# A three-layer graph network on one core: the order of the units in the third layer

## The chip, the cores and the metric

The kernel runs on one core of one Trainium2 chip. The metric is the device time in microseconds (us) of one execution. An execution is told by five engines that run side by side, each through its own list of instructions in order, and that wait for one another at semaphores: PE (TensorE, matmuls), DVE (VectorE), ACT (ScalarE), POOL (GpSimd, which here also issues the indirect DMAs) and SP (SyncE, which issues the plain DMAs).

## The reference

A graph of 20,000 nodes with 512 features each and 5,000 edges, sorted by their destination. Three layers of the same form, then the input is added back and normalized:

```python
h, residual = x, 0.0
for Wl, bl, Wr, g, b in params:          # three layers, weights 512 x 512
    msg = h[src]
    s = segment_sum(msg, dst)
    agg = s / maximum(cnt, 1.0)
    h = residual + agg @ Wl.T + bl + h @ Wr.T
    h = layer_norm(h, g, b)
    h = where(h >= 0, h, a_prelu * h)
    residual = h
out = layernorm(x + h)
```

## The kernel before, in words

The rows of a layer lie in 157 tiles of 128 rows (NT). Edge slots fill the first 40 tiles (ET): at most 127 edges each, so only these 40 tiles need the sum over messages. Tiles are worked through in pairs, called units: 20 **edge units** and 59 **plain units** (the last of them has one tile), 79 units a layer (UL), 237 in all. The list ORDER gives the sequence of a layer's units, the same in all three layers: 20 plain units (LEAD), then nineteen times an edge unit with two plain units behind it, then the last edge unit and the plain unit of one tile. In this text a unit's **position** is its place in its layer, 0 to 78, and "the row of position p" is the time on PE from the first transpose of that unit to the first transpose of the next.

Every engine walks over a counter T, the number of a unit, and does its part for units near T. The lists are written out by hand, so the order on an engine is fixed:

- PE (`tensor_program`): `turn` transposes the unit ahead (T+1) into ps_t (L373, 8 transposes for two tiles). Then `sum_messages` for tile 0 of the unit ahead if it is an edge unit (L385), `product_self` of tile 0 of unit T (L393, 12 matmuls), `sum_messages` for tile 1, `product_self` of tile 1, and for an edge unit `product_mean` for both tiles (L393, 12 matmuls each on sT). A plain unit is 8 transposes and 24 matmuls, an edge unit has 16 summing matmuls and 24 matmuls more.
- ACT (`scalar_program`): `square` of the second tile of T-1 (L499), `variance` (L509), `take_high` of T+1 (L490, from ps_t), in the third layer `out_norm` of T-4 (L552), `fill` of the bias into ps_z for T+1 (L519), in the third layer `out_square` of T-3 (L545), then `take_sum_high` of an edge unit (L528) and `square` of the first tile of T.
- POOL (`gpsimd_program`): `root` (L650, a power, and in the third layer L654 for the output), in the third layer `put_out` of T-5, two indirect DMAs that write the output (L662), then `gather_x`, `gather_messages` of T+3 if that is an edge unit (two indirect DMAs of 128 rows, L639).
- DVE (`vector_program`): `prelu` and in the third layer `out_sum` of T-3 (L784, L826), `take_sum_low` (L818), `carry` and `take_low` of T+1 (L745), `out_mean` (L833), `normal` and `add_shift` of T-1 (L757, L778), and `compare` for an edge unit at T+3 (L793, L795).
- SP (`sync_program`): `load_h` of T+3 (L283), `load_residual` in the third layer (L311), `load_rowtab` of T+5 (L293), `store_h` of T-3 (L300).

What ties them: `turn` of a unit waits until DVE has taken the low part of the one before it out of ps_t (`low`), `product_self` waits for `fill`, `fill` and `out_norm` stand behind one another on ACT, and `out_norm` waits for the L654 of POOL in the same step:

```python
act.wait_ge(o_move, u.pos + 1)      # out_norm, ACT
pool.wait_ge(o_done, u.o_ahead + j + 1)   # put_out, POOL
pe.wait_ge(m_in[j], 16 * (u.eno + 1))     # sum_messages, PE
```

The messages of layers two and three are gathered from the h that the layer before has stored in DRAM; `gather_messages` of the first edge unit of a layer waits until all of it is stored.

Of the kernel before, what the change touches and what calls it, by code (L numbers as in the profile page):

```python
# [15 lines left out]
L = 3  # L16
# [12 lines left out]
def build_program(nc, x, wT, bl, g, b, a_prelu, ident_in, const_in, edge_cols_in, edge_last_in, edge_rows_in,  # L29
# [5 lines left out]
    NT = -(-(N + ET) // P)  # L35
# [3 lines left out]
    edge_units = [(t, t + 1) for t in range(0, ET, 2)]  # L39
    plain_units = [tuple(range(t, min(t + 2, NT))) for t in range(ET, NT, 2)]  # L40
    UL = len(edge_units) + len(plain_units)
    UNITS = L * UL


    LEAD = len(plain_units) - 2 * len(edge_units) + 1
    assert LEAD >= 20
    ORDER = plain_units[:LEAD]
    for i, tiles in enumerate(edge_units):
        ORDER += [tiles, *plain_units[LEAD + 2 * i:min(LEAD + 2 * i + 2, len(plain_units) - 1)]]
    ORDER += plain_units[-1:]  # L50
    assert len(ORDER) == UL
    AHEAD = [sum(len(t) for t in ORDER[:i]) for i in range(UL)]
    EDGE_AT = [l * UL + ORDER.index(tiles) for l in range(L) for tiles in edge_units]

    class Unit:

        def __init__(self, no):
            self.no = no
            self.exists = 0 <= no < UNITS
            if not self.exists:  # L60
                return
            self.l, self.pos = divmod(no, UL)
            self.tiles = ORDER[self.pos]
            self.n = len(self.tiles)
            self.edge = self.tiles[0] < ET
            self.ahead = NT * self.l + AHEAD[self.pos]
            self.upto = self.ahead + self.n
            self.r2, self.r3 = no % 2, no % 3

            self.eno = len(edge_units) * self.l + self.tiles[0] // 2  # L70
            self.ring, self.lap = self.pos % OB, self.pos // OB
            self.o_ahead, self.o_upto = self.ahead - NT * (L - 1), self.upto - NT * (L - 1)

    def uses(ring, n, below):

        return len(range(ring, below, n))
# [7 lines left out]
    with ExitStack() as ctx:  # L84
# [3 lines left out]
        def sem(name):  # L88
            return ctx.enter_context(nc.semaphore(name))


        OB = 6
# [80 lines left out]
        edge_no, first, run = room[1][:, 0:P], room[1][:, P:2 * P], room[1][:, 2 * P:3 * P]  # L173
# [29 lines left out]
        BATCHES = -(-ET // BATCH)  # L203
        KNOWN_SLOT = [EDGE_AT[BATCH // 2 * b] - 4 for b in range(BATCHES)]

        EARLY, HALF = 18, 11
        NODE_SLOT = [2 + t if t < EARLY else EDGE_AT[(t - EARLY) // 2] + 1 + t % 2 for t in range(ET)]
        PLACES = EDGE_AT[1:HALF] + [T + i for T in EDGE_AT[HALF:len(edge_units)] for i in range(3)] + [UL, UL + 1, UL + 2]
        PUT_SLOT = PLACES[:ET]
# [3 lines left out]
        SRC_AHEAD = 6  # L213
        assert all(NODE_SLOT[t] < KNOWN_SLOT[t // BATCH] < PUT_SLOT[t] for t in range(ET)) and TABLE_SLOT + 3 < LEAD - 1 and PUT_SLOT[0] > TABLE_SLOT + 4
        assert len(PUT_SLOT) == ET and PUT_SLOT[-1] + 2 < EDGE_AT[len(edge_units)] - SRC_AHEAD

# [32 lines left out]
        o_put = [[sem(f"o_put{i}_{j}") for j in range(2)] for i in range(OB)]  # L249
# [3 lines left out]
        def rows(dram, u):  # L253
            return dram[P * u.tiles[0]:P * (u.tiles[0] + u.n), :].rearrange("(j p) d -> p j d", p=P)


        def sync_program(sp):
# [17 lines left out]
            def load_h(u):  # L275
                if u.l == 0:
                    return
                source = u.no - UL
                sp.wait_ge(turned, u.no - 2)
                sp.wait_ge(h_stored[source % 3], 16 * (source // 3 + 1))  # L280
                if u.no - 3 < UL:
                    sp.wait_ge(xp_stored[u.r3], 16 * uses(u.r3, 3, UL))
                sp.dma_start(hin[u.r3][:, 0:u.n, :], rows(h_dram[u.l - 1], u)).then_inc(h_in[u.r3], 16)  # L283
# [47 lines left out]
            for T in range(-5, UNITS + 3):  # L331
                for stage_, ahead in ((store_x, 2), (load_h, 3), (load_residual, -1), (load_rowtab, 5), (store_h, -3)):
                    u = Unit(T + ahead)
                    if u.exists:
                        stage_(u)
                for w, at in W_SLOT.items():
                    if T == at - 4:
                        load_weight(w)
                if T == TABLE_SLOT + 2:
                    sp.wait_ge(table_done, 3)  # L340
                    sp.dma_start(slot_dram[0:P * P, :].rearrange("(t p) c -> t (p c)", p=P),
                                 table_int[:, 0, :]).then_inc(slot_stored, 16)
                    sp.dma_start(slot_dram[P * P:NT * P, :].rearrange("(t p) c -> t (p c)", p=P),
                                 table_int[0:NT - P, 1, :]).then_inc(slot_stored, 16)
# [123 lines left out]
        def scalar_program(act):  # L468
# [52 lines left out]
            def take_sum_high(u, j):  # L521
# [3 lines left out]
                if u.eno > 0:  # L525
                    before = Unit(EDGE_AT[u.eno - 1])
                    act.wait_ge(z_ready, before.ahead + j + 1)
# [71 lines left out]
        def gpsimd_program(pool):  # L599
# [68 lines left out]
            for T in range(-3, UNITS + 6):  # L668
# [5 lines left out]
                for stage_, ahead in ((gather_x, 3), (gather_messages, 3), (find_source, SRC_AHEAD)):  # L674
                    u = Unit(T + ahead)
# [18 lines left out]
                        add_diagonal(w)  # L694
            for ring in range(OB):
                for j in range(2):
                    pool.wait_ge(o_put[ring][j], 16 * len([p for p in range(ring, UL, OB) if len(ORDER[p]) > j]))  # L697


        def vector_program(dve):  # L700
# [256 lines left out]
        with nc.Block() as block:  # L957
            block.sync(sync_program)
            block.tensor(tensor_program)
            block.scalar(scalar_program)  # L960
            block.gpsimd(gpsimd_program)
            block.vector(vector_program)
# [57 lines left out]
```

## Time and profile before

| | us |
|---|---|
| median of 3 runs | 2044.36 (2043.84 to 2045.36) |
| profiled execution, its own time | 2046.63 |
| profiled execution, span from first to last instruction | 2044.8 |
| PE busy | 1978.4 (97%) |
| DVE busy | 1601.2 (78%) |
| ACT busy | 1212.6 (59%) |
| POOL busy | 929.1 (45%) |

The span begins with set-up of tables and ends with the drain of the last units. The first transpose of the third layer stands at 1352.3 us. The busy time of PE is an upper figure, since matmuls overlap and their ends are modelled; the number to read is the time from a unit's first transpose to the next one's. In a timeline row the bracket at the end gives how long the engine stood idle before it and who released it.

### The profile page before, as it was taken

The page shows a single profiled execution, that of the slowest core. Times are in us where ns is not written, and L with a number is a line of the kernel's source. Part 1 is how long each engine was busy: PE and PEld are TensorE (multiplying, and loading weights), DVE is VectorE, ACT ScalarE, POOL GpSimd, SP SyncE. Part 2 cuts the span into 40 slices and gives each one's busy share as a digit, 9 for nine tenths or more (in the row PEclk, how much of TensorE's full clock was granted, in tenths as well). Part 3 has the DMA queues.
Part 4 walks back from the last instruction along what each step waited for, and adds up shares of the span by engine and source line. Part 5 has one row for each costly group of instructions (what it writes and reads, how often), then busy time and mean ns, then how long its engine had stood idle before and what let it go on. Part 6 is the DMA issues. An engine that isn't in the chain of part 4 may idle for free. (4 is left out here: it accounts for less than half of the span.)

```text
span 2044.8 us, 30402 instructions
## 1 busy us (share of the span) xinstructions
PE 1978.4 (97%) x10149; PEld 1653.5 (81%) x10149; DVE 1601.2 (78%) x2619; ACT 1212.6 (59%) x2643; POOL 929.1 (45%) x885
## 2 busy tenths in 40 slices
PE   6899999999999999999999999999999999999993
PEld 4778888888888888888888888887788888888882
DVE  7668787777777777777777777779998888888884
ACT  3775545555444455544444444458877777777774
POOL 2566655555665321233333333214555545555554
PEclk8999999999999999999999999999999999999997
DMA  5567676666666565444444444455666655566652
GB/s 185 179 214 270 206 228 227 209 224 211 206 207 200 170 170 171 165 155 155 155 145 147 152 155 155 135 176 197 228 223 211 214 208 206 211 216 213 210 186 90
DMA packets 181073, 387.66 MB, mean 190 GB/s; under 512 B 20117, under 2 KB 20562, under 8 KB 180918
## 3 DMA queue, kind: packets, MB, share of 16 engines
q1 hardware_dynamic: 142358, 272.06, 39.4%
q0 software_dynamic: 38560, 113.67, 17.3%
q8 instruction: 81, 1.33, 0.3%
q14 instruction: 74, 0.61, 0.1%
HBM read 221.07 MB, written 164.79 MB: 189 GB/s over the span
## 5 line engine op out<-in xcount | busy, mean ns | idle before, releaser
L393 PE MATMUL ps_z<-w_hi,hT_hi 128*128 128x512 f32 x1884 | 764.5, 406 | 5.2 <-ACT ps_z L519 5.0
L393 PE MATMUL ps_z<-w_hi,hT_lo 128*128 128x512 f32 x1884 | 739.8, 393 | 0.0
L393 PE MATMUL ps_z<-w_lo,hT_hi 128*128 128x512 f32 x1884 | 739.1, 392 | 0.0
L650 POOL TENSOR_TENSOR rstd<-veps,minus_half 128x2 f32<-128x2 f32 (+1 forms) x240 | 239.9, 1000 | 890.1 <-ACT veps L509 890.0
L745 DVE TENSOR_TENSOR hT_lo<-ps_t,hT_hi 128x1024 fp32r<-128x1024 f32 (+1 forms) x237 | 287.9, 1215 | 341.3 <-ACT hT_hi L490 338.7
L519 ACT COPY ps_z<-bias_rows 128x512 f32<-128x512 f32 x471 | 276.8, 588 | 370.1 <-DVE y L757 359.6
L499 ACT ACTIVATE junk<-ps_z 128x512 f32<-128x512 f32 x471 | 277.9, 591 | 318.8 <-PE ps_z L393 318.6
L393 PEld LDWEIGHTS ps_z<-w_hi,hT_lo 128*128 128x128 f32 x1884 | 354.1, 188 | 78.9
L393 PEld LDWEIGHTS ps_z<-w_hi,hT_hi 128*128 128x128 f32 x1884 | 355.4, 189 | 74.5 <-issue 8.1
L393 PEld LDWEIGHTS ps_z<-w_lo,hT_hi 128*128 128x128 f32 x1884 | 355.6, 189 | 66.8
L757 DVE SCALAR_TENSOR_TENSOR y<-ps_z,rstd,gain 128x512 f32<-128x512 f32 x471 | 330.1, 742 | 4.5 <-POOL rstd L650 4.5
L784 DVE SCALAR_TENSOR_TENSOR hout<-y,slope 128x1024 f32<-128x1024 f32 (+1 forms) x237 | 301.4, 1272 | 0.0
L778 DVE TENSOR_TENSOR y<-y,shift 128x1024 f32<-128x1024 f32 (+1 forms) x237 | 290.4, 1225 | 8.1
L373 PEld LDWEIGHTS ps_t<-ident,hin 128*128 128x128 f32 x1884 | 220.5, 141 | 38.6 <-issue 8.9
L373 PE MATMUL ps_t<-ident,hin 128*128 128x128 f32 x1884 | 246.6, 274 | 4.7 <-DVE hT_lo L745 4.7
L490 ACT CAST hT_hi<-ps_t 128x1024 fp32r<-128x1024 f32 (+1 forms) x237 | 234.6, 990 | 19.4 <-PE ps_t L373 19.2
L662 POOL DMA_INDIRECT out<-o_sb,node_put x157 | 165.3, 1053 | 68.2 <-issue 53.3
L616 POOL DMA_INDIRECT hin<-in_x,node_get x157 | 157.1, 1001 | 69.8 <-issue 36.2
L393 PE MATMUL ps_z<-w_hi,sT_lo 128*128 128x512 f32 x480 | 188.2, 392 | 0.0
L393 PE MATMUL ps_z<-w_lo,sT_hi 128*128 128x512 f32 x480 | 187.9, 391 | 0.0
L393 PE MATMUL ps_z<-w_hi,sT_hi 128*128 128x512 f32 x480 | 187.9, 391 | 0.0
L810 DVE SCALAR_TENSOR_TENSOR sumT<-over,sumT,ps_s 128x128 f32<-128x128 f32 x468 | 130.9, 342 | 37.9 <-PE ps_s L385 37.8
(131 smaller groups left out, 1898.7 us busy)
## 6 DMA issues: line engine op xcount, KB each, us to landing
h_scratch<-hout SPq DMA_DIRECT2D x156, 512.0 KB, 3.4
hin<-h_scratch SPq DMA_DIRECT2D x156, 512.0 KB, 4.0
x_by_slot<-hin SPq DMA_DIRECT2D x78, 512.0 KB, 3.2
o_sb<-x_by_slot SPq DMA_DIRECT2D x78, 512.0 KB, 4.5
rowtab<-edge_row_table SPq DMA_DIRECT2D x60, 256.0 KB, 3.5
stage<-in_WrT SPq DMA_DIRECT2D x3, 1024.0 KB, 8.5
stage<-in_WlT SPq DMA_DIRECT2D x3, 1024.0 KB, 7.0
hin<-in_x,node_get POOLq DMA_INDIRECT x157, 3.6
```

The source lines that it names most:

```text
L373: mm = pe.transpose(ps_t[:, j, k * P:(k + 1) * P], hin[u.r3][:, j, k * P:(k + 1) * P], ident[:])
L393: mm = pe.matmul(acc, a[:, k, :], ww[:, k, :], start=False, skip_group_check=True, stop=stop and k == KC - 1 and a is a_lo)
L490: nc.scalar.copy(hT_hi[u.r2][:, 0:u.n].rearrange("p j k n -> p (j k n)"), ps_t[:, 0:u.n, :].rearrange("p j d -> p (j d)")).then_inc(high, 1)
L499: nc.scalar.activation(junk[j][:], ps_z[u.r2][:, j, :], ACT.Square, accum_out=ssq[u.r2][:, j:j + 1]).then_inc(squared, 1)
L519: nc.scalar.copy(ps_z[u.r2][:, j, :], bias_rows[:, u.l, :]).then_inc(filled, 1)
L616: pool.indirect_dma_start(hin[u.r3][:, j, :], None, x, bass.IndirectOffsetOnAxis(node_get[:, t:t + 1], 0)).then_inc(x_in[u.r3][j], 16)
L650: nc.gpsimd.tensor_tensor(rstd[(T - 1) % 2][:, at], veps[(T - 1) % 2][:, at], minus_half[:, at], ALU.pow).then_inc(rstd_done, 1)
L662: pool.indirect_dma_start(out, bass.IndirectOffsetOnAxis(node_put[:, t:t + 1], 0), o_sb[u.ring][:, j, :], None, bounds_check=N - 1, oob_is ...
L745: nc.vector.tensor_tensor(hT_lo[u.r2][:, 0:u.n].rearrange("p j k n -> p (j k n)"), ps_t[:, 0:u.n, :].rearrange("p j d -> p (j d)"), hT_hi[ ...
L757: nc.vector.scalar_tensor_tensor(y[u.r2][:, j, :], ps_z[u.r2][:, j, :], rstd[u.r2][:, j:j + 1], gain[:, u.l, :], ALU.mult, ALU.mult).then_ ...
L778: nc.vector.tensor_tensor(y[u.r2][:, 0:u.n, :], y[u.r2][:, 0:u.n, :], moved, ALU.add).then_inc(shifted, 1)
L784: nc.vector.scalar_tensor_tensor(hout[u.r3][:, 0:u.n, :], y[u.r2][:, 0:u.n, :], slope[:, 0:1], y[u.r2][:, 0:u.n, :], ALU.mult, ALU.max).th ...
```

## The change

Layers one and two keep their order. The third layer gets its own: 8 plain units, then each edge unit with two or three plain units behind it in turn (E P P, E P P P, ten times), then the plain unit of one tile. The positions of edge units go from 20, 23, 26 ... 77 to 8, 11, 15, 18 ... 74. Since the same tile now stands at other positions in layers two and three, `load_h` looks up at which unit number the layer before made it (MADE_AT), and AHEAD becomes a list for each layer.

```diff
+    def order(lead):
+        left, among = len(plain_units) - lead - 1, len(edge_units)
+        first = [lead + max(min(2 * i, left), left * i // among) for i in range(among + 1)]
+        units = plain_units[:lead]
+        for i, tiles in enumerate(edge_units):
+            units += [tiles, *plain_units[first[i]:first[i + 1]]]
+        return units + plain_units[-1:]
+
     LEAD = len(plain_units) - 2 * len(edge_units) + 1
     assert LEAD >= 20
-    ORDER = plain_units[:LEAD]
...
+    ORDERS = [order(LEAD)] * (L - 1) + [order(8)]
+    AHEAD = [[sum(len(t) for t in units[:i]) for i in range(UL)] for units in ORDERS]
+    MADE_AT = [{tiles[0]: l * UL + pos for pos, tiles in enumerate(units)} for l, units in enumerate(ORDERS)]
+    EDGE_AT = [MADE_AT[l][tiles[0]] for l in range(L) for tiles in edge_units]
...
-            self.tiles = ORDER[self.pos]
+            self.tiles = ORDERS[self.l][self.pos]
...
-            self.ahead = NT * self.l + AHEAD[self.pos]
+            self.ahead = NT * self.l + AHEAD[self.l][self.pos]
...
-                source = u.no - UL
+                source = MADE_AT[u.l - 1][u.tiles[0]]
```

Three places on the engines show what moves. First POOL at the start of the third layer; L650/L655 is the root, L654/L659 the move for the output, L662/L667 puts a unit out (the number after o_sb is the position modulo 6), L639/L644 gathers the messages of an edge unit, one DMA a tile. Before, the first gather of the layer stands behind the thirteenth put, that of position 12:

```order
L650 TENSOR_TENSOR rstd1<-veps1,minus_half 128x4
L654 TENSOR_TENSOR omove1<-oneg1,rstd1 128x2
L662 DMA out<-o_sb0,node_put 20000x512 x2
L639 DMA msg0<-h2_scratch,src_slot 128x512
L639 DMA msg1<-h2_scratch,src_slot 128x512
```

With the change it stands behind the first put, that of position 0:

```order
L655 TENSOR_TENSOR rstd0<-veps0,minus_half 128x4
L659 TENSOR_TENSOR omove1<-oneg1,rstd0 128x2
L667 DMA out<-o_sb0,node_put 20000x512 x2
L644 DMA msg0<-h2_scratch,src_slot 128x512
L644 DMA msg1<-h2_scratch,src_slot 128x512
L655 TENSOR_TENSOR rstd1<-veps1,minus_half 128x4
```

The gather of the first edge unit has moved up by twelve units. Second, POOL further on, from the second gather of the third layer to the third. Before, three groups of root, move and put stand between any two gathers:

```order
L639 DMA msg1<-h2_scratch,src_slot 128x512
L650 TENSOR_TENSOR rstd1<-veps1,minus_half 128x4
L654 TENSOR_TENSOR omove2<-oneg2,rstd1 128x2
L662 DMA out<-o_sb1,node_put 20000x512 x2
...
L662 DMA out<-o_sb2,node_put 20000x512 x2
...
L662 DMA out<-o_sb3,node_put 20000x512 x2
L639 DMA msg0<-h2_scratch,src_slot 128x512
```

With the change there are four at this place, and three at the next:

```order
L644 DMA msg1<-h2_scratch,src_slot 128x512
L655 TENSOR_TENSOR rstd0<-veps0,minus_half 128x4
L659 TENSOR_TENSOR omove5<-oneg5,rstd0 128x2
L667 DMA out<-o_sb4,node_put 20000x512 x2
...
L667 DMA out<-o_sb5,node_put 20000x512 x2
...
L667 DMA out<-o_sb0,node_put 20000x512 x2
...
L667 DMA out<-o_sb1,node_put 20000x512 x2
L644 DMA msg0<-h2_scratch,src_slot 128x512
```

The gather belongs to the unit three places on, so where three plain units follow an edge unit it stands behind the step of the first plain one, and where two follow, behind the step of the edge unit. Third, ACT at the end of PE's work, the step of the last unit but one. Before, that unit's neighbour is an edge unit, whose message sums are cast (L528) between the squares:

```order
L528 CAST sT_hi<-sumT 128x512
L499 ACTIVATE junk,ssq<-ps_z 128x512
L528 CAST sT_hi<-sumT 128x512
L499 ACTIVATE junk,ssq<-ps_z 128x512
L509 ACTIVATE veps<-ssq,eps 128x4
L490 CAST hT_hi<-ps_t 128x512
```

With the change the last four units are plain ones:

```order
L550 ACTIVATE stage,ssq<-o_sb,oneg 128x512 x2
L524 COPY ps_z<-bias_rows 128x512
L504 ACTIVATE junk,ssq<-ps_z 128x512 x2
L514 ACTIVATE veps<-ssq,eps 128x4
L495 CAST hT_hi<-ps_t 128x512
```

The casts of the message sums have gone from the end of ACT's list; its number of instructions is the same.

## Rows read from the trace of the kernel before

**Rows 1.** The page, busy time, share of the span and instructions of PE.
```profile
PE 1978.4 (97%) x10149; PEld 1653.5 (81%) x10149; DVE 1601.2 (78%) x2619; ACT 1212.6 (59%) x2643; POOL 929.1 (45%) x885
```

**Rows 2.** Busy time by stretch: us; PE, PEld, DVE, ACT, POOL; PEclk, DMA, GB/s.
```profile
763.70:827.10 63.40, 63.40 (x321) 53.35 (x320) 49.55 (x52) 36.95 (x80) 12.19 (x16) 1.00 0.52 179
1407.40:1478.60 71.20, 66.76 (x322) 52.87 (x321) 64.85 (x101) 63.02 (x141) 37.49 (x41) 1.00 0.68 225
1486.20:1498.20 12.00, 9.91 (x48) 8.56 (x49) 10.55 (x18) 10.53 (x23) 6.43 (x8) 0.86 0.78 298
1516.40:1524.50 8.10, 8.10 (x49) 7.11 (x48) 7.96 (x18) 6.98 (x16) 3.59 (x4) 1.00 0.65 225
1524.50:1536.30 11.80, 11.80 (x57) 9.84 (x56) 11.40 (x22) 7.91 (x18) 7.12 (x6) 1.00 0.58 182
1536.30:1542.66 6.36, 6.36 (x33) 5.34 (x32) 4.17 (x6) 5.58 (x12) 3.27 (x4) 1.00 0.77 258
1542.70:1963.10 420.40, 420.40 (x2177) 356.82 (x2176) 376.58 (x705) 327.74 (x705) 221.91 (x224) 1.00 0.61 210
```

**Rows 3.** PE's timeline, first transposes of positions 7, 20 and 21: start us, us.
```profile
1394.44 1.03 PE L373 MATMUL ps_t<-ident,hin 128*128 128x128 f32 x8
...
1486.16 1.07 PE L373 MATMUL ps_t<-ident,hin 128*128 128x128 f32 x8 [0.25 <-DVE hT_lo L745]
1489.32 2.05 PE L385 MATMUL ps_s<-same,msg 128*128 128x128 f32 x8 [2.09 <-issue]
...
1491.59 0.63 PE L393 MATMUL ps_z<-w_lo,hT_hi 128*128 128x512 f32 x1
...
1498.24 1.03 PE L373 MATMUL ps_t<-ident,hin 128*128 128x128 f32 x8
```

**Rows 4.** Waits from 1401 to 1500 us: us in total, times, longest us.
```profile
ACT o_sb L552 <- POOL omove L654: 11.7, 13, 2.7
...
PE ps_z L393 <- ACT ps_z L519: 5.0, 11, 0.7
```

**Rows 5.** ACT's timeline, start us, us, in for positions 7, 16 and 17.
```profile
1397.75 1.00 ACT L490 CAST hT_hi<-ps_t 128x1024 fp32r<-128x1024 f32 x1
...
1462.00 1.00 ACT L490 CAST hT_hi<-ps_t 128x1024 fp32r<-128x1024 f32 x1
...
1469.23 1.00 ACT L490 CAST hT_hi<-ps_t 128x1024 fp32r<-128x1024 f32 x1
```

**Rows 6.** POOL's timeline, first put's end and the first gather of layer three.
```profile
1394.27 0.98 POOL L662 DMA_INDIRECT out<-o_sb,node_put  x1 [0.30 <-issue]
...
1482.24 1.98 POOL L639 DMA_INDIRECT msg<-h_scratch,src_slot  x1 [0.30 <-issue]
...
1485.73 1.07 POOL L650 TENSOR_TENSOR rstd<-veps,minus_half 128x4 f32<-128x4 f32 x1
```

**Rows 7.** Line L639, landing of its DMAs: the first two of layer three.
```profile
DMA to landing us min/median/max: 6.8/6.9/7.0
```

**Rows 8.** Line L639, landing of its DMAs: the other 38 of layer three.
```profile
DMA to landing us min/median/max: 3.4/4.2/5.6
```

**Rows 9.** POOL's timeline, second plain unit of one block.
```profile
1540.87 0.98 POOL L662 DMA_INDIRECT out<-o_sb,node_put  x1 [0.30 <-issue]
1544.57 1.39 POOL L650 TENSOR_TENSOR rstd<-veps,minus_half 128x4 f32<-128x4 f32 x1 [2.72 <-ACT veps L509]
```

**Rows 10.** ACT's timeline at the same place.
```profile
1537.43 0.99 ACT L490 CAST hT_hi<-ps_t 128x1024 fp32r<-128x1024 f32 x1
...
1544.39 0.99 ACT L490 CAST hT_hi<-ps_t 128x1024 fp32r<-128x1024 f32 x1
```

**Rows 11.** ACT's timeline at the end, its last wait for PE.
```profile
2009.10 0.60 ACT L499 ACTIVATE junk<-ps_z 128x512 f32<-128x512 f32 x1 [2.03 <-PE ps_z L393]
...
2009.82 0.30 ACT L509 ACTIVATE veps<-ssq,eps 128x4 f32<-128x4 f32 x1
```

**Rows 12.** PE's timeline, its last matmul.
```profile
2011.40 0.39 PE L393 MATMUL ps_z<-w_hi,hT_lo 128*128 128x512 f32 x1
```

More of the change, by code:

```diff
@@ L42, in build_program @@
     UNITS = L * UL
+    def order(lead):
[5 more added lines that the diff above has]
+        return units + plain_units[-1:]
     LEAD = len(plain_units) - 2 * len(edge_units) + 1
     assert LEAD >= 20
-    ORDER = plain_units[:LEAD]
[L48 to L53, printed above, removed]
+    ORDERS = [order(LEAD)] * (L - 1) + [order(8)]
+    AHEAD = [[sum(len(t) for t in units[:i]) for i in range(UL)] for units in ORDERS]
+    MADE_AT = [{tiles[0]: l * UL + pos for pos, tiles in enumerate(units)} for l, units in enumerate(ORDERS)]
+    EDGE_AT = [MADE_AT[l][tiles[0]] for l in range(L) for tiles in edge_units]
     class Unit:
@@ L696, in gpsimd_program @@
                 for j in range(2):
-                    pool.wait_ge(o_put[ring][j], 16 * len([p for p in range(ring, UL, OB) if len(ORDER[p]) > j]))
+                    pool.wait_ge(o_put[ring][j], 16 * len([p for p in range(ring, UL, OB) if len(ORDERS[L - 1][p]) > j]))
         def vector_program(dve):
```

## The prediction

> **What bounds the kernel now.** I read the page first: PE is busy for 1978.4 of 2044.8 us [rows 1], so the most that any order can give is the time in which PE waits or runs slowly. Next I read the table of busy time by stretch, cut at first transposes. Ten plain units of the second layer take 63.4 us with PE busy throughout, 6.34 us each; ten plain units of the third layer, positions 9 to 18, take 71.2 us, 7.12 us each, with PE busy for 66.8 of them; one block of an edge unit and two plain ones in the third layer takes 8.1 + 11.8 + 6.4 = 26.3 us, and the next sixteen blocks take 420.4, again 26.3 each, all with PE busy throughout [rows 2]. So the third layer is bound by PE once edge units are mixed in, and by something else in its run of plain units.
>
> What that is: in the run ACT is busy for 63.0 us of ten units and DVE for 64.9, 6.30 and 6.49 a unit, both near PE's 6.34. The engines wait besides: ACT's `out_norm` (L552) waited for POOL (L654) 13 times, 11.7 us in all, 0.9 a unit, and PE waited for ACT's `fill` (L519) 11 times, 5.0 us in all [rows 4]. ACT's work and its wait make 7.2 a unit, and its timeline shows that step: from one `take_high` to the next it is 7.23 us [rows 5]. That is the bound: ACT in order, with a wait for POOL inside. In a block with an edge unit ACT is busy for 7.0 + 7.9 + 5.6 = 20.5 us of 26.3 and DVE for 8.0 + 11.4 + 4.2 = 23.5 [rows 2], so even with 0.9 of waiting in each of three steps ACT has 3 us to spare, which is what a later plain unit can use.
>
> **What is removed.** The first transpose of position 7 starts at 1394.44, that of position 20, the first edge unit, at 1486.16 [rows 3]: 91.7 us for 13 plain units, which at 6.34 would be 82.4. Excess: **9.3 us**. The row of position 20 lasts from 1486.16 to 1498.24, 12.1 us, where an edge row later takes 8.1 [rows 2, 3]. Excess: **4.0 us**, and it has two halves: 2.09 us of waiting ahead of the summing matmuls (L385), and slow matmuls right behind it, 0.63 instead of 0.39 us [rows 3]; the granted clock of the stretch is 0.86 of full [rows 2], part of it at 1.2 instead of 2.4 GHz. The wait is for the messages: POOL issued the gather at 1482.24, the DMAs landed 6.8 to 7.0 us after issue, which is 1489.2, and PE started at 1489.32 [rows 3, 6, 7]. Together 13.3 us. Positions 0 to 6 keep their order, and show no excess worth counting. All other rows of the layer already run at PE's rate.
>
> **What is added or moved.** No instruction is added; PE's, ACT's, DVE's, POOL's and SP's work is the same in number. Four places can cost.
>
> *The first edge unit, now at position 8.* The lag of ACT behind PE has grown to 1397.75 - 1394.44 = 3.3 us at position 7 [rows 3, 5], and PE is not yet held by it. POOL's first put ends at 1394.27 + 0.98 = 1395.25; the gather comes 0.3 later, at 1395.55 [rows 6]. With 7.0 us of landing the messages are there at 1402.6. PE asks for them after the transposes of position 8, at 1394.44 + 6.34 + 0.9 = 1401.7. That is a wait of **0.9 us** in place of 2.1; with the later gathers' 4.2 us of landing [rows 8] it would be none. The gathers keep POOL for 3.5 us (1482.24 to 1485.73, [rows 6]), so the next root is about 1.4 late and ACT with it; PE then stands in a row of 8.1 and one of 11.8 us, which take up most of that. I add 0.3. Sum **+1.2**; bounds 0 and all of the old price of this place, 4.0 with its slow matmuls and 1.2 of delay in the row ahead, 5.2. I take a value near the lower end, because the first gather's own row gives 0.9 and because behind a wait of half the length I expect no slow matmuls.
>
> Here a page of the Trainium skill bears on the sum. "DMA: Bandwidth & Descriptors", section "Anatomy of one DMA", gives a GpSimd DMA about 2.0 us plus its bytes over 436 GB/s, 2.6 us for these 256 KB as an estimate; by it the messages would be there early and this place would cost 0.3 instead of 1.2. The trace does not agree: the median here is 4.2 and the first two took 6.8 and 7.0 [rows 7, 8], so I keep the rows.
>
> *The ten blocks with three plain units.* The third plain unit brings a step of 7.1 to 7.2 us against a row of 6.34, so it adds 0.8 of lag. In the block shown, `take_high` stands 1537.43 - 1536.30 = 1.1 us behind the first transpose of the second plain unit and 1544.39 - 1542.66 = 1.7 behind that of the next unit [rows 2, 10]. In these blocks the gather also moves to the step of the first plain unit: POOL ends its put at 1541.85 [rows 9], the gather's 0.3 and 3.5 us end at 1545.65, and the root which started at 1544.57 [rows 9] starts 1.1 late. The lag at the third plain unit becomes 1.7 + 1.1 = 2.8, under the 3.3 that did not hold PE, and the edge row of 8.1 and the row of 11.8 behind it take it away. The messages: issued at 1542.15, with 4.2 us of landing there at 1546.4, with 7.0 at 1549.2; PE asks at 1542.66 + 6.34 + 0.9 = 1549.9. So **0**; bounds 0 and 0.5 a block (the mean of PE's waits for `fill`, 5.0 / 11, [rows 4]), 5 in all. I take the lower end, for the margins of 0.5 and of 0.7 us or more. What hides both is that margin of one row of PE.
>
> *Loads, row tables and h.* SP's loads of h look up the same or an earlier position of layer two for plain tiles, and one 3 to 12 later for edge tiles, which is stored by then too: an edge unit of position 8 was made at position 20 of 79. The row table of the first edge unit is asked for five units ahead as before. DVE's comparing for it falls into the run, 1 us where DVE idles 0.6 a unit (7.12 less 6.49, [rows 2]); counted in the 0.3 above. Cost 0.
>
> *The end.* Before, the last unit but one is an edge unit. ACT waits for its product (2.03 us, [rows 11]) and starts `variance` (L509) at 2009.82; PE's last matmul ends at 2011.79 [rows 11, 12], 2.0 later, and 33.0 us remain from there to the end. Now the last rows are three plain ones behind one of 11.8. ACT's lag there is 1.1, 1.7 and, at the last unit, 2.5; its step of 7.1, less 0.6 for the one-tile unit, puts that `variance` 2.3 + 6.5 = 8.8 us behind the last first transpose, while PE needs 0.5 + 5.4 + 2.7 = 8.6. So `variance` starts 0.2 after PE's end instead of 2.0 before it, and the drain is longer by **+2.1**. Bounds 0 (the drain hangs on POOL alone) and 4 (one more us in each of two steps).
>
> **Sum.** -13.3 + 1.2 + 0 + 0 + 2.1 = **-10.0 us**. Against the profiled execution: span 2044.8 to 2034.8, its own time 2046.6 to 2036.6. The median of the runs lies 2.3 under that execution's own time, so the forecast is 2044.4 - 10.0 = **2034.4 us**.
>
> **Rivals.** A measurement of this kernel can tell about 0.2%, 4.1 us, from no change.
>
> (a) *All is gained*: the messages land in 4.2 us and the drain is no longer, -13.3: 2031.1. For it: 38 of 40 gathers landed within 5.6 us. Against it: the first pair is the one moved, and the step of 7.1 at the end.
>
> (b) *POOL's late root is passed on.* If each of the ten longer blocks passes its 1.1 us and the third unit's 0.8 to PE, and nothing takes them up, the price is 19 us: 2053. Halfway (only what exceeds the margin of 0.5) it is 10 x 1.4 = 14: 2048, within 0.2%. Against it: DVE and ACT idle for 2 us and more in every block. With a few tenths a block it gives 2037 to 2040.
>
> (c) *The slower one: the messages come late in the longer blocks.* The gather there has 7.7 us from issue to PE's asking, 12 in the shorter ones. If the landing took 9.8 us, PE would wait 2.1 and run slowly behind each wait, 4.0 a block as at position 20: 40 less 10, 2074. It is slower from 1.0 us a block, a landing over 8.7. Against it: 5.6 is the longest of 38 and 7.0 of all [rows 7, 8]. For the slow matmuls behind each wait speaks the rule in "TensorE: Matmul & The Clock Gate" of the Trainium skill, section "HAM oscillation": repeated waits for a DMA send PE back to its slower clock each time. The row of 0.63 us agrees for the one wait here.
>
> (d) *The run is slow wherever it stands*: the time that ACT and POOL need for 59 plain units is only moved. Then nothing is won: 2044. Against it: the sixteen blocks with PE never idle.
>
> **How the numbers follow.** Forecast, 2032.5 to 2037: 0.55. (a): 0.15. (b) in tenths, 2037 to 2040.2: 0.14; (b) in full or (d), within 0.2%: 0.09. (b) at its worst or (c), slower by over 0.2%: 0.04; a gain beyond (a), 0.03. So faster 0.87, same 0.09, slower 0.04. The range takes in (a), and on the other side the bounds of the first edge unit (4 more) and part of the end: 2030.9 to 2039.5.
>
> **What would show it.** Positions 8 to 18 of the third layer in rows of 6.34, 8.1 and 11.8 us, with the one wait ahead of L385 under 1.5 us and no matmuls of 0.63 behind it; blocks of 26.3 and 32.6 us; PE's last matmul 12 us earlier; a drain of 35 us. The forecast is wrong if PE waits for `fill` or for messages in the longer blocks, or if the drain is 33 us or over 37.

## The result, and the profile after

The changed kernel takes 2036.35 us in the median of 6 runs (2035.68 to 2037.35) against 2044.7 of the kernel before (2043.84 to 2046.96); the ratio is 0.9956, 95% interval 0.9946 to 0.9967. That is 8.35 us less where 10.0 was forecast, inside the range. The profiled executions differ by more: the span falls from 2044.8 to 2033.9, by 10.9 us.

Of the page of the changed kernel, the line that answers to [rows 1]:

```profile
PE 1973.3 (97%) x10149; PEld 1651.9 (81%) x10149; DVE 1600.5 (79%) x2619; ACT 1212.3 (60%) x2643; POOL 929.4 (46%) x885
```

The busy table of the changed kernel, columns as in [rows 2]: the first edge unit's row (position 8), the row behind it, one block of an edge unit and three plain ones, and everything from the first transpose of position 11 to that of position 74:

```profile
1400.64:1409.17 8.53, 8.42 (x50) 7.21 (x50) 7.92 (x13) 7.96 (x17) 4.86 (x5) 1.00 0.75 272
1409.17:1420.97 11.80, 11.80 (x57) 9.84 (x56) 11.63 (x23) 10.36 (x24) 6.42 (x7) 1.00 0.63 216
...
1427.30:1460.00 32.70, 32.70 (x170) 27.67 (x169) 29.00 (x54) 25.76 (x57) 16.64 (x18) 1.00 0.57 198
...
1427.30:1957.50 530.20, 530.20 (x2738) 449.43 (x2737) 482.33 (x883) 425.85 (x922) 284.71 (x289) 1.00 0.64 215
```

PE is never idle from position 11 to position 74, and the granted clock is full throughout. The block of four units (positions 11 to 14) takes 32.7 us, which is 26.3 and one row of 6.35. The first edge unit's row is 8.53 us long where 8.14 is PE's own. I added up, for each row from the first transpose of position 1 to that of position 78, what it takes above PE's own time (6.35; 1.79 more for an edge unit's summing; 5.44 more behind an edge unit). The sum is 13.5 us in the kernel before and 0.8 after: **12.7 us gone**. The drain, from the end of PE's last matmul to the end of the span, grew from 33.1 to 34.4 us: **1.4 us given back**. The two make 11.3. The third layer also began 0.2 us earlier, and the row of position 78, which the sum leaves out, is 0.5 us longer than PE's own, most of it a wait for `fill`; that makes the 10.9 of the spans. The wait:

```profile
1996.48 0.47 PE L398 MATMUL ps_z<-w_hi,hT_hi 128*128 128x512 f32 x1 [0.28 <-ACT ps_z L524]
```

The messages at position 8, on PE and on POOL of the changed kernel:

```profile
1400.64 1.05 PE L378 MATMUL ps_t<-ident,hin 128*128 128x128 f32 x8
1401.52 1.06 PE L390 MATMUL ps_s<-same,msg 128*128 128x128 f32 x8
```

```profile
1395.42 1.00 POOL L644 DMA_INDIRECT msg<-h_scratch,src_slot  x1 [0.30 <-issue]
1396.73 1.91 POOL L644 DMA_INDIRECT msg<-h_scratch,src_slot  x1 [0.30 <-issue]
1398.65 1.58 POOL L655 TENSOR_TENSOR rstd<-veps,minus_half 128x4 f32<-128x4 f32 x1
```

PE sums the messages at once: the wait of 2.09 us of [rows 3] is gone, not halved. The gather begins at 1395.42, where the prediction put it (1395.55), and PE asks 6.1 us later. The first of the two gathers landed 3.5 us after its issue, the second 8.1; PE asks for the second one 4.0 us after the first. What is left of 0.4 us stands behind ACT, whose `out_norm` waited for the root that the gather had held up:

```profile
1400.55 1.52 ACT L557 ACTIVATE o_sb<-o_sb,omove,rstd 128x512 f32<-128x512 f32 x2 [1.93 <-POOL omove L659]
```

In the longer blocks POOL's step is the forecast one. The gather and the root behind it in the first of these blocks (positions 11 to 14; the messages are those of position 15), and ACT's wait for the root:

```profile
1453.18 1.02 POOL L644 DMA_INDIRECT msg<-h_scratch,src_slot  x1 [0.30 <-issue]
1454.50 1.91 POOL L644 DMA_INDIRECT msg<-h_scratch,src_slot  x1 [0.30 <-issue]
1456.43 1.58 POOL L655 TENSOR_TENSOR rstd<-veps,minus_half 128x4 f32<-128x4 f32 x1
```

```profile
1458.32 1.52 ACT L557 ACTIVATE o_sb<-o_sb,omove,rstd 128x512 f32<-128x512 f32 x2 [1.93 <-POOL omove L659]
```

ACT waits 1.93 us in place of 0.88, 1.05 more (1.1 forecast), and PE does not notice. The time from the gather's issue to PE's first summing matmul is 7.8 us in the longer blocks (7.6 in the first) and 10.5 behind the shorter ones (9.3 behind the first); in the kernel before it was 11.8 nearly everywhere. Landing, of the 38 gathers behind the first pair, took 4.2 us in the median, 8.6 at most:

```profile
DMA to landing us min/median/max: 3.4/4.2/8.6
```

In the kernel before the longest behind the first pair was 5.6 us [rows 8]. The long ones now belong to the second gather of a pair: in the first three of the longer blocks the first gather landed in 3.4 to 3.6 us and the second in 8.3 to 8.6. PE asks for the second 4 us later than for the first, so neither made it wait.

At the end, ACT's `variance` and PE's last matmul, to be read beside [rows 11, 12]:

```profile
1998.97 0.30 ACT L514 ACTIVATE veps<-ssq,eps 128x4 f32<-128x4 f32 x1
```

```profile
1999.06 0.39 PE L398 MATMUL ps_z<-w_hi,hT_lo 128*128 128x512 f32 x1
```

`variance` starts 0.5 us before PE's end; before it was 2.0 before it. That is 1.5 us, and the drain is 1.4 longer.

### The profile page after: what moved, and what is told of

It reads as the page before. It is cut to its first block and busy times, and to the rows that moved or that the text cites. A ratio compares the mean times of both kernels' runs of the same rounds, so it can differ in the third digit from the quotient of the medians.

```text
span 2033.9 us, 30402 instructions
## 1 busy us (share of the span) xinstructions
PE 1973.3 (97%) x10149; PEld 1651.9 (81%) x10149; DVE 1600.5 (79%) x2619; ACT 1212.3 (60%) x2643; POOL 929.4 (46%) x885
## 5 line engine op out<-in xcount | busy, mean ns | idle before, releaser
L655 POOL TENSOR_TENSOR rstd<-veps,minus_half 128x2 f32<-128x2 f32 (+1 forms) x240 | 240.4, 1002 | 881.2 <-ACT veps L514 881.0
L667 POOL DMA_INDIRECT out<-o_sb,node_put x157 | 167.3, 1066 | 66.5 <-issue 49.8
L557 ACT ACTIVATE o_sb<-o_sb,omove,rstd 128x512 f32<-128x512 f32 x157 | 119.6, 809 | 74.6 <-POOL omove L659 74.6
```

What stands on the lines that cost most here:

```text
L655: nc.gpsimd.tensor_tensor(rstd[(T - 1) % 2][:, at], veps[(T - 1) % 2][:, at], minus_half[:, at], ALU.pow).then_inc(rstd_done, 1)
L667: pool.indirect_dma_start(out, bass.IndirectOffsetOnAxis(node_put[:, t:t + 1], 0), o_sb[u.ring][:, j, :], None, bounds_check=N - 1, oob_is ...
```

## The experiments

There were twelve runs, two of them of the unchanged kernels for comparison, and one a repeat. Theory A is the prediction's: ACT's step of 7.1 us, in order and with the wait for POOL inside, holds PE in a run of plain units, and the first edge unit pays 4 us when it comes at the end of such a run. Theory B puts all of the gain on the first edge unit.

**The run's length: 14 plain units first.**

```diff
-    ORDERS = [order(LEAD)] * (L - 1) + [order(8)]
+    ORDERS = [order(LEAD)] * (L - 1) + [order(14)]
```

> The changed kernel with 14 plain units ahead of the first edge unit of the third layer in place of 8. Theory A (the run: from position 8 on each plain unit ahead of the first edge unit costs PE some 0.7 us, because ACT's step of 7.1 us exceeds PE's row of 6.34, and the first edge unit costs up to 4 us more when it comes at the end of such a run): rows of 7.0 to 7.3 us at positions 9 to 13, 4.4 us of excess there, and 1 to 4 us at the first edge unit; 5 to 8 us over the changed kernel's 2036.4, so 2041.5 to 2044.5. Theory B (the gain is only the first edge unit's wait and slow matmuls, which come after a long run and grow with it): about 2036 to 2038.5, rows of the run near 6.4.

Measured: 2043.71 us (ratio to the kernel before 0.9987, 0.9977 to 0.9997). The stretch of positions 9 to 13, then the first edge unit's row, with PE's wait in it:

```profile
1407.95:1444.04 36.09, 33.47 (x162) 26.43 (x161) 33.50 (x54) 30.90 (x70) 20.58 (x21) 1.00 0.67 225
1444.04:1454.75 10.71, 8.42 (x49) 7.18 (x49) 9.23 (x14) 9.19 (x20) 6.38 (x8) 1.00 0.75 275
```

Five rows take 36.1 us, 7.2 each, as forecast by A (7.0 to 7.3); the summed excess is 7.5 us, 4.6 of it at positions 8 to 13 and 2.6 at the first edge unit. B, which expects rows near 6.4, falls: 6.8 us of excess come back with six plain units, of 12.7. The time, 7.4 us above the changed kernel's 2036.35 in another job, agrees.

**5 plain units first.** The same edit with 5.

> The changed kernel with 5 plain units first in place of 8. Theory A: positions 0 to 7 have no excess in either order, so there is nothing to gain but the 0.4 us of position 8; the first gather now stands where POOL must wait for the last stores of layer two, which can hold the roots by 1 to 4 us. Within 2 us of the changed kernel, PE's rows from position 5 on at its rate with at most 2 us of excess at positions 3 to 6.

Measured: 2036.10 us (0.9959, 0.9944 to 0.9974), beside 2036.19 of the changed kernel in the same job. The excess is 0.4 us, all at position 1. The 0.4 of position 8 is gone, the first gather did not hold PE visibly (1360 to 1400 us has PE busy for 40.0), and there was nothing else to win. That agrees with the prediction's reading that positions 0 to 7 cost nothing worth counting.

**The first edge unit alone.** In the kernel before, the first gather of the third layer is issued three units earlier.

```diff
-                for stage_, ahead in ((gather_x, 3), (gather_messages, 3), (find_source, SRC_AHEAD)):
+                for stage_, ahead in ((gather_x, 3), (gather_messages, 3), (gather_messages, 6), (find_source, SRC_AHEAD)):
                     u = Unit(T + ahead)
                     if u.exists:
+                        first = u.l == L - 1 and u.tiles[0] == 0
+                        if stage_ is gather_messages and first != (ahead == 6):
+                            continue
                         stage_(u)
```

> The kernel before, with one edit: the gather of the first edge unit of the third layer is issued six units ahead in place of three. Theory A: the wait of 2.1 us at the first edge unit and the slow matmuls behind it (1.9 us) go, but the run of 9.3 us stays, and the gather's 3.5 us on POOL now delay one root inside the run, 1 to 2 us; 2 to 4 us under the kernel before, 2040.5 to 2042.5. Theory B: 8 us under the kernel before, near 2036.5.

Measured: 2043.46 us (0.9983, 0.9974 to 0.9993), against 2046.64 in that job. Positions 9 to 18, and the row of position 20:

```profile
1408.31:1479.41 71.10, 66.77 (x322) 52.89 (x321) 64.71 (x101) 63.05 (x141) 41.57 (x43) 1.00 0.72 233
1486.97:1495.15 8.18, 8.18 (x48) 7.16 (x49) 8.04 (x13) 7.28 (x17) 4.37 (x5) 1.00 0.70 247
```

That is 3.2 us less, where A had 2 to 4; the time itself lies above the 2040.5 to 2042.5 expected, since the kernel before stood at 2046.64 in this job and not at 2044.7. The first edge unit's excess is gone whole, 4.0 us, clock and all, and the run's is untouched: ten rows take 71.1 us, in [rows 2] 71.2. The summed excess is 9.5. So the two terms of the prediction, 9.3 and 4.0, have these sizes, and the second can be taken away without the first. The delay of a root that I had expected inside the run did not show; the two gathers took POOL 1.0 us each here.

**ACT's wait filled.** In the kernel before, `square` of the first tile stands right behind `take_high` in positions 5 to 18, and no longer at the end of the step.

```diff
+                early = u.exists and u.l == L - 1 and 5 <= u.pos < LEAD - 1
+                if early:
+                    square(u, 0)
                 old = Unit(T - 4)
                 if old.exists:
                     out_norm(old, 0)
...
-                if u.exists:
+                if u.exists and not early:
                     square(u, 0)
```

> The kernel before, with one edit: for positions 5 to 18 of the third layer ACT squares the first tile of its unit right behind take_high, ahead of out_norm, where it waits for POOL 0.5 to 0.9 us now, in place of at the end of its step. The work is the same. Theory A (ACT in order with the wait for POOL inside sets 7.1 us): the step falls to DVE's 6.5 us, rows of the run of 6.5 in place of 7.1, 5 to 7 us under the kernel before, 2037.5 to 2040. Rival (DVE, busy for 6.49 us a unit, with its own waits sets the row): the row stays within 0.2 us of 7.1, and the time within 1.5 us of 2044.7.

Measured: 2037.49 us (0.9952, 0.9935 to 0.9969). Positions 12 to 18, seven rows:

```profile
1426.99:1473.13 46.14, 45.87 (x225) 37.45 (x224) 44.82 (x71) 44.50 (x99) 24.21 (x29) 1.00 0.74 245
```

ACT's timeline in one of these steps:

```profile
1463.69 1.00 ACT L490 CAST hT_hi<-ps_t 128x1024 fp32r<-128x1024 f32 x1
1464.59 0.60 ACT L499 ACTIVATE junk<-ps_z 128x512 f32<-128x512 f32 x1
...
1465.42 1.52 ACT L552 ACTIVATE o_sb<-o_sb,omove,rstd 128x512 f32<-128x512 f32 x2
...
1470.20 1.00 ACT L490 CAST hT_hi<-ps_t 128x1024 fp32r<-128x1024 f32 x1
```

The same work in another order: the step from `take_high` to the next is 6.51 us in place of 7.23 [rows 5], the row is 6.59, `out_norm` waits 0.2 us at most where it waited up to 1.0 (1405 to 1476 us: 1.4 us in all, 7.6 before). The summed excess falls from 13.5 to 3.4 us. This is the direct test: what held PE in the run was ACT's wait for POOL inside its own order, not DVE, though DVE (6.40 us a row here) is near to being the next. A expected 5 to 7 us under the kernel before, and it is 9.2. The surplus is the first edge unit, which A had left out: its excess fell from 3.9 to 0.4 us, though its gather still stands in the same place on POOL. Without the lag PE asked for the messages 6.1 us after their issue in place of 5.0; they landed in 5.7 and 6.9 us where it had been 6.8 and 7.0, and PE did not wait:

```profile
1480.32 1.06 PE L373 MATMUL ps_t<-ident,hin 128*128 128x128 f32 x8 [0.48 <-DVE hT_lo L748]
1481.21 1.06 PE L385 MATMUL ps_s<-same,msg 128*128 128x128 f32 x8
```

So the 4.0 us at position 20 were not independent of the run: its lag had taken 1.1 us off the lead of the messages. The first landing was also 1.1 us shorter here; which of the two weighs more was not tried. The edit alone, with the old order of units, comes within 1.1 us of the changed kernel; by the ratios to the kernel before in each one's job, 0.9952 and 0.9956, the two can't be told apart.

**The kernel before once more**, for its spread.

> The kernel before, unchanged, profiled once more, since its first profiled execution took 1.9 us more than its median. If the run of plain units is set by ACT's step, its rows of positions 8 to 19 differ by less than 0.5 us in sum from the first profile; if the first edge unit's price depends on when its messages land, the difference of the two executions lies in that row, 0 to 4 us.

Measured: 2048.22 us in its profiled execution. The rows of positions 8 to 19 sum to the same excess within 0.2 us, and position 20 again waits (2.28 us) and runs slowly; its row too differs by only 0.2 us:

```profile
1409.03:1480.30 71.27, 66.96 (x323) 53.07 (x323) 64.86 (x101) 63.22 (x141) 39.73 (x41) 1.00 0.68 224
1487.53:1499.86 12.33, 10.05 (x49) 8.41 (x50) 10.84 (x19) 10.82 (x24) 6.47 (x8) 0.86 0.76 287
```

The span is 1.6 us longer than the first one, and 1.5 of that lie ahead of the third layer, whose first transpose starts at 1353.9 in place of 1352.3.

**How many plain units one edge unit can carry.** The changed kernel with other blocks (`blocks` lays the given number of plain units behind each edge unit in turn).

```diff
+    def blocks(lead, behind):
+        units, at = plain_units[:lead], lead
+        for tiles, n in zip(edge_units, behind):
+            units += [tiles, *plain_units[at:at + n]]
+            at += n
+        assert at == len(plain_units) - 1
+        return units + plain_units[-1:]
...
-    ORDERS = [order(LEAD)] * (L - 1) + [order(8)]
+    ORDERS = [order(LEAD)] * (L - 1) + [blocks(8, [2] * 14 + [3, 4, 5, 6, 2, 2])]
```

> The changed kernel with 8 plain units first and then 2 plain units behind each of fourteen edge units, 3, 4, 5 and 6 behind the next four, 2 behind the last two. Theory A (each plain unit beyond the second adds 0.75 us of lag of ACT behind PE; PE is held from a lag of some 4 us on; the gather's delay of 1 to 1.4 us on POOL counts once a block): no excess in the blocks of 3 and 4, under 0.5 us in all in the block of 5, 0.5 to 2 us in the block of 6 with its following edge unit. Time within 2 us of the changed kernel. Rival (every third plain unit costs, hidden in the rows): the excess grows from the block of 3 on.

Measured: 2038.42 us (0.9968, 0.9957 to 0.9979). No excess in the block of three. Behind four plain units the next edge unit's row has 0.4 us, behind five 0.3. Behind six, the sixth plain unit's row has 0.6 and the next edge unit's 0.7, where PE's `turn` waited for DVE's low part:

```profile
1932.38:1939.30 6.92, 6.62 (x34) 5.25 (x32) 6.78 (x14) 5.15 (x14) 5.80 (x6) 1.00 0.55 182
1939.30:1948.10 8.80, 8.66 (x48) 7.15 (x49) 8.63 (x16) 8.23 (x17) 5.00 (x6) 1.00 0.70 268
```

2.0 us in all; A's figures but for the block of four, where it had none. Up to five plain units behind an edge unit cost PE at most 0.4 us in all; with the sixth it is 1.2 us, and more than six were not tried. Three of the seven runs took 2041.9 to 2042.8 us, the other four 2037.5 to 2038.4; the profile is of the lowest, so what the three lost stays open.

**The end.** The same function with `blocks(8, [50 * (i + 1) // 19 - 50 * i // 19 for i in range(19)] + [0])`: the layer ends with an edge unit and the one-tile unit again.

> The changed kernel (8 plain units first) with the 50 plain units laid behind nineteen edge units, two or three each, and none behind the last edge unit, so that the layer ends as in the kernel before: edge unit, plain unit of one tile. Theory A (the drain grew by 1.4 us because ACT's variance of the last step no longer waits for the edge unit's product but ends after PE): drain of 33.1 us in place of 34.5, all rows still at PE's rate, so 1.4 us under the changed kernel, 2034 to 2036. Rival (the drain depends on POOL's indirect DMAs alone): no difference, drain of 34.5.

Measured: 2035.08 us (0.9941, 0.9928 to 0.9955), drain 32.9 us, excess 0.75. Repeated beside the changed kernel on one chip:

> edge_last once more beside the changed kernel on one chip. Theory A: 1.0 to 2.0 us under it, all of it in the drain (33.0 against 34.5 us).

> The changed kernel, unchanged, on the chip of the next run, to be compared with it: 0.9940 to 0.9967 of the kernel before.

Measured: 2034.13 us (2033.13 to 2034.82; 0.9949, 0.9935 to 0.9962) against 2036.19 (2035.92 to 2037.36; 0.9961, 0.9947 to 0.9975); drains of 32.9 and 34.4 us, excess 0.8 in both. ACT waits for PE again before its last but one `variance`:

```profile
1997.05 0.60 ACT L512 ACTIVATE junk<-ps_z 128x512 f32<-128x512 f32 x1 [2.00 <-PE ps_z L406]
1997.78 0.30 ACT L522 ACTIVATE veps<-ssq,eps 128x4 f32<-128x4 f32 x1
```

So the drain's growth belongs to the order of the last units. The gap of the medians, 2.1 us, is 0.6 more than the drain shows. The traces have these 0.6 us too: from the first transpose of position 78 to PE's end the changed kernel takes 9.4 us and this one 14.2, or 8.8 without the product of its edge unit (5.44); in the changed kernel PE waits 0.3 us there for `fill`. The ranges do not overlap. This version is faster than both kernels.

**A slower POOL, in both orders.** The root is run twice, the first time into a spare buffer, in each step that also serves the output; the results don't change.

```diff
+                if old.exists:
+                    nc.gpsimd.tensor_tensor(spare[(T - 1) % 2][:, at], veps[(T - 1) % 2][:, at], minus_half[:, at], ALU.pow)
                 nc.gpsimd.tensor_tensor(rstd[(T - 1) % 2][:, at], veps[(T - 1) % 2][:, at], minus_half[:, at],
                                         ALU.pow).then_inc(rstd_done, 1)
```

> The kernel before, with POOL's root (the power, 1.04 us and more) run a second time into a spare buffer ahead of the real one in each step that also serves the output, so that ACT's out_norm waits 1.05 us more. Theory A: rows of the run of plain units 8.1 to 8.3 us in place of 7.1, some 13 us, the blocks of edge, plain, plain at most 0.3 us longer each (ACT: 20.5 + 3 x 1.95 = 26.35 against 26.3), the drain 5 us longer: 18 to 25 us over the kernel before. Rival (DVE or the output DMAs set the row of 7.1): rows within 0.3 us of 7.1 and only the drain longer, 5 us.

Measured: 2068.28 us (1.0106, 1.0090 to 1.0121). The run's rows, ten of them, and one block behind it:

```profile
1413.92:1492.68 78.76, 66.76 (x321) 52.86 (x321) 64.81 (x101) 63.22 (x140) 46.30 (x51) 1.00 0.60 203
1537.86:1564.32 26.46, 26.46 (x137) 22.32 (x136) 24.13 (x45) 20.36 (x45) 17.16 (x17) 1.00 0.67 217
```

Rows of 7.88 us in place of 7.12: the run does hang on the wait for POOL, though 1.04 us of root gave only 0.76, less than the 8.1 to 8.3 us a row that A had. The block hardly moves. The summed excess is 26.0 against 13.5, the drain 37.2 against 33.1.

> The same edit in the changed kernel. Theory A: blocks with two plain units 26.3 to 26.6 us, blocks with three about 33.8 in place of 32.65 (ACT: 26.1 + 4 x 1.95), 11 us in ten of them, 1 to 3 us at the first edge unit and 5 in the drain: 15 to 22 us over the changed kernel. If the mixed order had slack for any wait of this size: only the drain, 5 us.

Measured: 2071.55 us (1.0123, 1.0108 to 1.0139), 3 us slower than the old order with the same root, and 35 us over the changed kernel where A had 15 to 22. A's figure is missed, and so is its rival's. The excess of the rows grew by 23.4 us, the drain by 2.7, the last row by 4.0, and 5.4 lie ahead of the third layer. PE's waits from 1400 to 2000 us, and one of the places:

```profile
PE ps_s L391 <- issue: 15.0, 9, 2.3
```

```profile
1530.61 1.03 PE L379 MATMUL ps_t<-ident,hin 128*128 128x128 f32 x8
1533.62 1.13 PE L391 MATMUL ps_s<-same,msg 128*128 128x128 f32 x8 [1.97 <-issue]
```

PE waits for messages at the first edge unit and in eight of the nine edge rows behind three plain units, hardly for `fill`. That is the prediction's slower rival (c), brought about by one microsecond more on POOL, and it comes about in two ways: PE asks 6.6 us after the issue in place of 7.8, and the first gather of the pair now lands in 8.4 us at the place shown, where it landed in 3.4 to 3.6 in the changed kernel. Why it lands so late was not tried; had it landed in 3.6 us, a lead of 6.6 would have been enough. To see whether these waits are the cause, the gather of the edge units behind three plain ones is issued four units ahead:

```diff
-                for stage_, ahead in ((gather_x, 3), (gather_messages, 3), (find_source, SRC_AHEAD)):
+                for stage_, ahead in ((gather_x, 3), (gather_messages, 3), (gather_messages, 4), (find_source, SRC_AHEAD)):
                     u = Unit(T + ahead)
                     if u.exists:
+                        if stage_ is gather_messages and u.edge and (ahead == 4) != after_three(u):
+                            continue
                         stage_(u)
```

> The changed kernel with the doubled root (as after_root2), and the gather of each edge unit that follows three plain units issued four units ahead in place of three. Theory A now (with a slower POOL the longer blocks lose to late messages: PE waited 15 us in 9 places ahead of the summing matmuls, up to 2.3 us each, and ran at the lower clock behind some): these waits vanish, the excess at positions 15, 22, 29 ... falls from 1.3 to 2.4 us to under 1, 10 to 16 us under after_root2, 2056 to 2062. Rival (the excess is ACT's step, 33.8 us a block, and the wait for messages only lies inside it): the waits move to fill (L519's fill of ps_z) and the time stays within 3 us of 2071.5.

Measured: 2058.89 us (1.0071, 1.0056 to 1.0087), 12.7 under the run before it, which was in another job; the spans differ by 12.3. PE's waits in the same stretch:

```profile
PE ps_z L399 <- ACT ps_z L525: 3.3, 10, 0.9
...
PE ps_s L391 <- issue: 2.1, 1, 2.1
```

One wait for messages is left, the first. The block with three plain units takes 32.8 us, not the 33.8 that A had from ACT's sum; that part of A, ACT's waits simply added up, is wrong. The likely reason is that a later root costs nothing where ACT waits for PE anyway: those waits of ACT came to 39.2 us from 1460 to 1980 us in the changed kernel and to 1.6 from 1465 to 1980 here. With this edit the mixed order keeps its lead over the old one under the slower POOL too, 2058.9 against 2068.3 (ratios 1.0071 and 1.0106).

## Why the prediction was right, point by point

- **What bounds the kernel**: right, and shown. ACT's step with its wait for POOL set the run's 7.1 us (square_early, before_root2), and the mixed rows had room.
- **What is removed, 9.3 + 4.0**: right. early_gather takes away the 4.0 and leaves 9.5 of excess; lead14 brings back 4.6 at six positions. What the prediction did not see is that the 4.0 depended on the run: square_early, which edits the run alone, takes away 3.5 of them too.
- **The first edge unit, +1.2**: measured 0.4. The term was too large because it took the landing time of 7.0 us from the one crowded place; here the first gather landed in 3.5 us. The second took 8.1, more than any before, and did no harm only because PE asks for it 4 us later, which the prediction left out. The estimate from the Trainium skill's page, "DMA: Bandwidth & Descriptors", section "Anatomy of one DMA", would have given 0.3 and came nearer, but its 2.6 us of landing are not what the trace shows: 4.2 in the median and 3.4 at the least. That no slow matmuls would follow was right.
- **The ten longer blocks, 0**: right to 0.02 us a row, with the root 1.05 us late (1.1 forecast) and 7.8 us of lead for the messages (7.7 forecast). The landings were not as forecast: the longest behind the first pair grew from 5.6 to 8.6 us, and the margin held because the slow one was the second of its pair. Rival (c) had the right weak point: it takes 1 us more on POOL to make it real.
- **The end, +2.1**: the drain grew by 1.4; `variance` came 0.5 us before PE's end where I had it 0.2 after. ACT was where the prediction put it, 8.85 us behind the last first transpose (8.8 forecast). PE was later: it took 9.3 us where 8.6 was forecast, 0.5 of that because it waited for ACT's `fill`, a wait that the prediction did not have. Drain and last row together cost 1.9, near the 2.1. (The working has ACT's lag as 2.5 us in one sentence and 2.3 in the next and does not say why; the sum goes by 2.3.) The mechanism is shown by edge_last, which undoes both.
- **The sum, -10.0**: by spans of the profiled executions -10.9, by medians -8.4, in the second job with the changed kernel 2044.7 to 2036.2, -8.5. The traces account for it: -12.7 in the rows, +1.4 in the drain, +0.5 in the last row, -0.2 ahead of the layer. The first edge unit's 0.8 less than forecast makes most of the difference to -10.0. That the medians differ by some 2.5 us less stays open. The kernel before spreads from 2042.9 to 2048.6 over all jobs, the changed one only from 2035.7 to 2037.4, and the two profiled executions of the kernel before both lay 1.6 us and more above their job's median. Part of the spread lies ahead of the third layer (the 1.6 us of before_again). Whether the slow matmuls at position 20 are missing in the executions that were not profiled can't be seen.

## What to carry to other kernels

Where one kind of work leaves the leading engine idle for a little per unit and another kind leaves room on the followers, lay them alternately from the first unit at which a lag has built up, and ask of the new order two things: what the last units leave for the drain, and what is issued a fixed number of units ahead, since its lead in time shrinks where the units between are short (11.8 to 7.8 us here). A wait that stands inside an engine's own order can also be filled: moving one instruction into it gave as much here as reordering the layer, within the noise. Whether the two together give more was not tried.

## What the runs showed of the hardware that was not expected

A wait of PE of some 2 us does not always bring the lower clock. At position 20 of the kernel before, waits of 2.1 and 2.3 us were followed by matmuls at half rate, granted clock 0.86 over the row, in both profiled executions. So was a wait of 2.1 us for `fill` in the last row of after_root2, behind rows in which PE had been busy throughout (1994.26 to 2018.90 us), and a wait of 2.2 us at the same place of root2_gather4. The row of after_root2:

```profile
2018.90:2032.23 13.33, 10.83 (x41) 8.08 (x39) 10.08 (x17) 9.59 (x25) 8.03 (x9) 0.87 0.36 124
```

In lead14 PE waited 2.3 us ahead of the first edge unit, and the clock stayed at 1.00, so the row's excess was 2.6 in place of 4.0. It stayed at 1.00 in the row of before_root2's first edge unit too, with a wait of 1.7 us behind thirteen rows that had each held PE for 0.9 to 1.2 us, and in all nine edge rows of after_root2 in which PE waited for messages, 1.0 to 2.3 us. So neither the length of the wait nor the number of held rows ahead of it tells these cases apart; what does stays open. (The expectation of root2_gather4 says that PE ran at the lower clock behind some of those waits; the rows do not show it.) Taking away all but one of the waits of after_root2 took 12.9 us off the waiting (15.0 to 2.1) and 11.7 off the rows' excess (24.2 to 12.4), so they cost no more than their own length. For rival (c) the prediction drew on "TensorE: Matmul & The Clock Gate" of the Trainium skill, section "HAM oscillation". The waits that this section describes are longer than any here, and the prediction carried them over to waits of 2.1 us. For those the runs show both outcomes, so the section does not bear out a price of slow matmuls behind each of them.

The second gather of a pair takes POOL 1.9 us in most places of both orders and 1.0 at the first edge unit of early_gather, for the same 128 rows; what it meets there was not tried. In the three kernels with a doubled root the third layer began at 1356.4 to 1357.6 us in place of 1352 to 1354, though the edit adds nothing ahead of it but a spare buffer; this too stays open, and 2 to 5 us of their times are not the root's.
